# Spreading projections, experts' outputs and combining over the row maxima's units, in a TensorE queue written out by hand

## The reference

```python
slots = einsum('bsd,bset->betd', xn, softmax(logits, axis=1))
processed = gelu(slots @ w1) @ w2
out = einsum('bnd,bsn->bsd', processed, softmax(logits.reshape(b, s, e*t)))
```

## Time and profile before

| | |
|---|---|
| median of 3 runs | 1322.0 us (1321.63 to 1325.11) |
| profiled execution's own time | 1320.49 us |
| its span, first to last instruction | 1318.7 us |
| mean granted TensorE clock | 0.938 of full |
| busy: TensorE, VectorE, ACT, GpSimd | 1137.4, 908.6, 641.3, 480.9 us |
| window 388.1 to 473.4 (slot 4) | TensorE busy 79.14 us, clock 1.00 |
| window 301.6 to 388.1 (slot 3) | TensorE busy 80.55 us, clock 0.98 |

### The profile page before, as it was taken

How to read it: one execution, slowest core, us unless ns; L and a number is a source line. 1 busy time by engine, 2 the same in 40 slices (tenths; PEclk the granted TensorE clock), 3 DMA queues, 4 the chain that set the end, 5 groups by cost and what they waited for, 6 DMA issues and landing times.

```text
span 1318.7 us, 19164 instructions
## 1 busy us (share of the span) xinstructions
PE 1137.4 (86%) x6056; PEld 603.7 (46%) x6056; DVE 908.6 (69%) x2097; ACT 641.3 (49%) x1258; POOL 480.9 (36%) x602
## 2 busy tenths in 40 slices
PE   5979889999898998989996851177999999999997
PEld 3434454553554544635444430133455555455453
DVE  3627537456588687786875577998799898898131
ACT  2161734726637457385373410333465556645642
POOL 3040311312334144252333243354537546556310
PEclk8989999899999999999899885588999999999999
DMA  4220110221322314124113058221020220200000
GB/s 116 71 90 32 49 64 10 74 73 35 113 67 69 111 33 146 42 49 134 47 37 73 20 143 204 69 51 37 22 67 17 51 67 8 58 24 8 25 9 8
DMA packets 86004, 79.84 MB, mean 61 GB/s; under 512 B 43056, under 2 KB 63664, under 8 KB 83888
## 3 DMA queue, kind: packets, MB, share of 16 engines
q1 hardware_dynamic: 85936, 79.01, 22.2%
HBM read 43.17 MB, written 35.00 MB: 59 GB/s over the span
## 4 chain that ended last, share of the span: by engine, by line
PE 60%; DVE 16%; issue 9%; ACT 8%; POOL 4%; DMA 2%; SPq 1%; ACTq 0%; DVEq 0%; POOLq 0%
PE ps L1348 15%; PE ps L1329 8%; PE ps L992 5%; PE ps L957 4%; PE ps L1031 4%; ACT arena L1482 3%; PE ps L995 3%; PE ps L1339 3%; PE ps L1002 3%; PE ps L1018 3%; ACT arena L1443 2%; DVE arena L1881 2%; PE ps L1060 2%; PE ps L1098 2%; PE ps L1080 2%
## 5 line engine op out<-in xcount | busy, mean ns | idle before, releaser
L1881 DVE TENSOR_REDUCE arena<-ps 128x4 f32<-128x512 f32 (+2 forms) x192 | 197.7, 1043 | 64.0 <-PE ps L995 60.9
L1348 PE MATMUL ps<-arena,late 128*128 128x512 f32 x512 | 227.1, 596 | 0.3 <-ACT arena L1631 0.3
L1443 ACT ACTIVATE arena<-ps 128x512 f32<-128x512 f32 (+2 forms) x200 | 110.4, 569 | 210.6 <-PE ps L957 99.0
L776 POOL TENSOR_SCALAR_AFFINE_SELECT arena<-arena 128x512 f32<-128x512 f32 x128 | 90.5, 710 | 265.9 <-ACT arena L1482 265.4
L1482 ACT ACTIVATE arena<-ps 128x1024 f32<-128x1024 f32 (+3 forms) x256 | 169.3, 713 | 31.0 <-PE ps L1018 29.7
L1348 PEld LDWEIGHTS ps<-arena,late 128*128 128x128 f32 x512 | 96.3, 192 | 114.4 <-issue 112.1
L1631 ACT ACTIVATE arena<-ps,f_s 128x512 f32<-128x512 f32 x128 | 83.3, 688 | 109.3 <-PE ps L1348 98.6
L1002 PE MATMUL ps<-mask_qk,ident_b 128*128 128x512 bf16 x388 | 103.9, 388 | 25.8 <-DVE arena L2165 25.8
L1443 ACT ACTIVATE arena<-ps,arena 128x128 f32<-128x128 f32 (+1 forms) x128 | 62.3, 528 | 120.6 <-DVE arena L1908 47.2
L957 PE MATMUL ps<-ident,arena 128*128 128x128 f32 (+1 forms) x624 | 102.2, 298 | 21.6 <-ACT arena L1443 12.6
L874 POOL TENSOR_TENSOR arena<-arena 128x256 f32<-128x256 f32 x128 | 93.5, 730 | 66.0 <-ACT e_w L1690 43.3
(11 more groups left out here) (187 smaller groups left out, 1941.7 us busy)
## 6 DMA issues: line engine op xcount, KB each, us to landing
qr<-q_rep SPq DMA_DIRECT2D x16, 512.0 KB, 5.0
kr<-k_rep SPq DMA_DIRECT2D x16, 512.0 KB, 5.9
scan_d<-late SPq DMA_DIRECT2D x56, 138.0 KB, 3.0
arena<-scan_d SPq DMA_DIRECT2D x12, 552.0 KB, 7.3
q_rep<-hilo SPq DMA_DIRECT2D x24, 256.0 KB, 3.2
k_rep<-hilo SPq DMA_DIRECT2D x24, 256.0 KB, 3.5
proj_d<-arena SPq DMA_DIRECT2D x8, 768.0 KB, 5.1
late<-proj_d SPq DMA_DIRECT2D x8, 768.0 KB, 4.4
```

Source lines behind the costliest of these rows:

```text
L776: g.affine_select(out=block, in_=block, compare_op=ALU.is_ge, fill=0.0, base=0, pattern=[[0, 4], [1, P]], channel_multiplier=-1).then_inc( ...
L1348: last = pe.matmul(ps[:, ring2.bank(f"{n}{c}"), :], w[:, k, c * P:(c + 1) * P], src[:, k, :], start=(k == 0), stop=(k == HC - 1))
L1443: return act.activation(dst, src(ps[:, bank, :]), func, **kw)
L1881: v.tensor_reduce(heads[:, 2 * pr:2 * pr + 2, gs[0]:gs[-1] + 1], ps[:, at:at + 2, 0:len(gs) * w].rearrange("p q (n w) -> p q n w", w=w), X ...
```

## The change

TensorE's end of a slot is driven by a table. `UNITS_TO` says how many units are issued ahead of each of twelve pieces: c0 behind x1, c1 behind x2, c2 behind x4, c3 behind x5, the four experts' outputs (now one block each) behind x7, x8, x10 and x11, the four blocks of combining behind x12, x13, x15 and x17. The transposes of the maxima stand behind x13 as before, those of x1 behind x15 (X_AT = 16), now with combining blocks 0 and 1 ahead of them and 2 and 3 behind. Unread matmuls are issued in this stretch only in a slot without a mixture. Banks 4 and 5 change places for part of the shared uses, and xT moves from 4 to 7. ACT issues the one-element exponential and `take_x1` ahead of `take_combined`.

```diff
--- before.py
+++ after.py
@@ -40,6 +40,8 @@
 QUARTER = NC // 4
 X_LATE = 19
 NM_AT, XR_AT = 13, 14
+X_AT = 16
+UNITS_TO = [2, 3, 5, 6, 8, 9, 11, 12, 13, 14, 16, 18]
 SCW = TS * 2 * HD + 2 * HD * TS + NC * 10
 PAIRS = [(r, r * (r + 1) // 2) for r in range(CH)]
 LN_EPS = 1e-5
@@ -471,10 +473,10 @@
         assert len(turns) % 2 == 0
 
 
-        shared = [(F, "xT", 4), (T, "L0", 5), (T, "L1", 7), (T, "L2", 4), (F, "qkv0", 5), (XE, beside[0], 7), (F, "qkv1", 4),
+        shared = [(F, "xT", 7), (T, "L0", 5), (T, "L1", 7), (T, "L2", 4), (F, "qkv0", 5), (XE, beside[0], 7), (F, "qkv1", 4),
                   (F, "qkv2", 5), (XE, beside[1], 7), (F, "qkv3", 4), (T, "L3", 5), (XE, beside[2], 7), (T, "M0", 4),
                   (T, "M1", 5), (XE, beside[3], 7), (T, "M2", 4), (T, "M3", 5)]
-        shared += [(hand, use, (7, 4, 5)[k % 3]) for k, (hand, use) in enumerate([
+        shared += [(hand, use, (7, 5, 4)[k % 3]) for k, (hand, use) in enumerate([
             (K, "nm1"), (T, "cT0"), (T, "cT1"), (F, "qT"), (F, "kT"), (T, "cT2"), (T, "cT3"), (N1, "pv0"), (T, "dT0"),
             (T, "dT1"), (T, "dT2"), (T, "dT3"), (T, "sn"), (N1, "pv1"), (T, "slots"), (N1, "pv2"), (T, "h0"), (N1, "pv3"),
             (T, "h1"), (N1, "aT"), (T, "h2"), (T, "h3"), (G, "x2T"), (N1, "ao"), (G, "c0"), (G, "c1"), (G, "c2"), (G, "c3"),
@@ -1238,33 +1240,27 @@
                     nonlocal x_at
                     while x_at < end:
                         if front is not None:
-                            if x_at > NM_AT or chain_only:
+                            if chain_only:
                                 idle_matmuls(2)
                             scores_for_maxima(front, f"x{x_at}", turn)
                         x_at += 1
 
-                maxima_to(2)
-                for j in range(4):
-                    if tail is not None:
-                        project(tail, turn, j)
-                    maxima_to(3 + j)
-                for half in range(2):
-                    if moe is not None:
-                        expert_out(moe, turn, (2 * half, 2 * half + 1))
-                    maxima_to(8 + 2 * half)
-                for t in range(NT):
-                    if moe is not None:
-                        combine(moe, turn, (t,))
-                    maxima_to(11 + t)
-                if front is not None:
-                    transpose_maxima(front, turn, 0)
-                maxima_to(X_LATE - 3)
-                if b is not None:
-                    if front is not None:
-                        idle_matmuls(2)
-                    transpose_x1(b, turn)
+                pieces = [lambda j=j: project(tail, turn, j) for j in range(4)] if tail is not None else [None] * 4
+                pieces += [lambda n=n: expert_out(moe, turn, (n,)) for n in range(4)] if moe is not None else [None] * 4
+                pieces += [lambda t=t: combine(moe, turn, (t,)) for t in range(NT)] if moe is not None else [None] * 4
+                filled = moe is not None
+                for end, piece in zip(UNITS_TO, pieces):
+                    maxima_to(end)
+                    if end == NM_AT + 1 and front is not None:
+                        transpose_maxima(front, turn, 0)
+                    if end == X_AT and b is not None:
+                        if front is not None and not filled:
+                            idle_matmuls(2)
+                        transpose_x1(b, turn)
+                    if piece is not None:
+                        piece()
                 maxima_to(X_LATE)
-                if front is not None:
+                if front is not None and not filled:
                     idle_matmuls(4)
                 return now
 
@@ -1605,10 +1601,11 @@
                     take_projections(tail)
                 if moe is not None:
                     take_expert_out(moe)
+                if b is not None:
+                    act.activation(warm[:, :], ident[:, 0:1], ACT.Exp)
+                    take_x1(b)
+                if moe is not None:
                     take_combined(moe)
-                if b is not None:
-                    take_x1(b)
-                    act.activation(warm[:, :], ident[:, 0:1], ACT.Exp)
 
             take_xT(0)
             for t in range(NT):
```

## The result

The changed kernel took 1330.68 us (median of 11 runs, 1324.53 to 1342.58); the kernel before took 1324.02 us in the runs beside it (11 runs, 1321.63 to 1332.95). The ratio is 1.0061, with a 95% interval of 1.0033 to 1.0090, so the change makes the kernel slower, by 4 to 12 us on 1324. The forecast was 5.0 us; the medians differ by 6.7 us. The changed kernel's median lies 3.7 us over the predicted 1327.0. The profiled execution spans 1328.9 us, 10.2 more than the one before.

A forecast was written before the change was run, and what follows sets the result against it. TensorE was taken to bound the slot's end, busy without a break. Terms -20.4 + 18.8 + 6.6 gave +5.0 us, 1327.0 on the median of 1322.0; own range 1323.5 to 1330, over all cases 1314 to 1333.

The forecast's parts named there:

- Unread matmuls removed and pieces respread: Ends of slots 1 to 6: 16 unread matmuls fewer on TensorE's chain, 3.4 us gained a slot, -20.4 us in all.
- nothing is lost by their absence as cover of the clock: End of slot 4: the clock stays up without the unread matmuls, because real matmuls fill the stretch; no cost.
- What becomes late: Start of slots 4 to 7: the fold waits for scale_heads behind GpSimd's add; 4.0 us in slots 4 to 6; sum +18.8.
- Products longer by 1.03 us: Fold's three VectorE products, slots 4 to 6: 2.72 us beside GpSimd's score_products instead of 1.69; TensorE's new wait 4.6 us.
- e21: TensorE's unit behind the fold, ahead of projections and scores: forecast to wait 4.6 us in slots 4 to 6, 5.0 in slot 7.
- The clock, 2.2 us a slot: Slots 4 to 6, behind TensorE's stop at e21: the clock falls to 0.50, 2.2 us each, +6.6 us.
- a rival with 0.11: Clock falls again in mid-slot in slots 4 to 6, or VectorE bounds the respread units: +10 to +12 us, chance 0.11.
- Slot 7 pays it already: Slot 7: its clock already falls before the change, so no clock cost added; its forecast loss is 5.0 us.
- Slots 1 to 3: These slots have no fold waiting and keep the whole gain of 3.4 us each.
- The prediction's 3.7 us: Fold's three products by the skill's whole-instruction exclusion: 3.7 us, sum 4 us worse; the prediction went by 2.72 instead.

## Why the prediction was right, and where its sizes were off

The direction and the mechanism held: the fold waits behind the add, TensorE waits behind the fold, the clock falls behind that, and it comes to more than the removal gains. The size came out near (5.0 us forecast, 4 to 12 measured), though 1330.68 lies just over the forecast's own range of 1323.5 to 1330, and in part it came out by luck: some terms were too large, others too small.

- *Unread matmuls removed and pieces respread, -3.4 us a slot.* From x0 to L0 the timelines give 28.18 and 24.84 us in slot 4: 3.34. But "nothing is lost by their absence as cover of the clock" holds only with the respreading; alone the removal loses the clock (1335.57 us). I had asked whether VectorE keeps up in the new order, not what the old order would do without them. The lighter L1816 was right: 1.1 us in slots where GpSimd's add no longer lies beside it.
- *What becomes late, 4.0 us at the fold.* Measured 3.70 (VectorE reached the fold 0.2 us later behind L0 than before, by small waits at the tops), and 4.26 in slot 7 (4.4 worked out). Taking the wait away turned the loss into a gain: shown.
- *Products longer by 1.03 us.* Mis-sized: 1.88 us in slots 4 to 6, only 0.19 more. In slot 7 they took 2.71, as the row of slot 7's end said. The two steps behind them (0.90 and 0.74 us instead of 0.41 and 0.42) lie beside two instructions of GpSimd's L778 here, and TensorE doesn't wait for them. By the timelines e21 starts 12.29 us behind L0 in slot 4 instead of 8.38, a delay of 3.91 us, not 4.6; in slot 7 13.61 instead of 8.64, 4.97 us, as forecast.
- *The clock, 2.2 us a slot.* By the profiles the fall behind the stop costs 2.4 us a slot (the kernel with 16 matmuls). But I had put the second fall, 17 us later, into a rival with 0.11, and it came in all three slots. Its price is about 1 us a slot, as an estimate: the slots lost 11.8 us, and 3 × (3.91 + 2.4 - 3.34) = 8.9 of it are the terms above. "Slot 7 pays it already" was wrong too: its clock was low 20.5 us instead of 6.8, and the slot lost 7.1 us, not 5.0, although TensorE's delay there was as forecast.
- *Slots 1 to 3* gained 9.4 of 10.2 us, but not by 3.4 each: slot 1 gained nothing, its clock was low for 20.4 us instead of 6.8, and slot 2 gained 6.8, as its clock didn't fall any more, after 13.6 us low. That the three add up to the forecast is luck.

Why the fold's products took 1.88 us and not 2.72 shows when VectorE's and GpSimd's are taken one by one. In slot 4 of the changed kernel:

```profile
387.22 0.29 DVE L1989 TENSOR_TENSOR late<-late 128x128 f32<-128x128 f32 x1 [3.70 <-POOL late L804]
387.26 0.56 POOL L815 TENSOR_TENSOR late<-late 128x128 f32<-128x128 f32 x1
387.43 0.68 DVE L1989 TENSOR_TENSOR late<-late 128x256 f32<-128x256 f32 x1
387.79 0.91 POOL L815 TENSOR_TENSOR late<-late 128x256 f32<-128x256 f32 x1
388.03 1.08 DVE L1989 TENSOR_TENSOR late<-late 128x384 f32<-128x384 f32 x1
388.65 1.30 POOL L815 TENSOR_TENSOR late<-late 128x384 f32<-128x384 f32 x1
```

They end in turn (387.51, 387.82, 388.11, 388.70, 389.11, 389.95), each stretched by the one before it on the other engine. VectorE starts first here, by 0.04 us, and its first product is free (0.29 us); in slot 7 GpSimd starts first, by 0.03 us (655.03 against 655.06), VectorE's first product takes 0.58 us, and the three wait for three of GpSimd's instead of two. This agrees with the Trainium skill's exclusion for a whole instruction (SBUF — State Buffer, Who interferes with whom). The prediction's 3.7 us worked out from it, an estimate, was too high all the same. GpSimd's four products grow from 128 to 512 elements a partition; their mean, 0.83 us, was taken for the three shortest, which took 0.45, 0.73 and 0.99 us in the kernel before, and in slots 4 to 6 only two of them stand in VectorE's way.

The sum by slots: -9.4 (1 to 3; -10.2 forecast), +11.8 (4 to 6; +10.2 forecast), +7.1 (7; +5.0 forecast), so +9.4 between the L0 of slot 1 and of slot 8, in one profile of each kernel. Why the clock falls in some slots and holds in others with the same pauses I can't say from these runs; single profiles differ by several us in slots 0 and 1 for this alone.

## What to carry to other kernels

When work is moved later on one engine to balance it, follow its result through every queue behind it: here an add that had been harmless in GpSimd's queue carried an unrelated stage's five products with it, and reordering that queue turned a loss of 0.6% into a gain of 0.5%. Before unread matmuls are taken out, ask what TensorE will do in their place: if it waits, they may hold the clock, and the best kernel here took them out where real work fills the gap and put five in where nothing does.

## What the runs showed of the hardware

- In the kernel with the removal alone the granted clock fell from 1.00 to 0.50 at the ends of slots 1 to 6 with no stop of TensorE longer than 1.20 us in those ends (at the end of slot 4 its pauses were 1.11, 0.47, 0.47 and 0.21 us). The prediction's clock term counted only the fall behind a stop of several us.
- VectorE's and GpSimd's products, two operands in SBUF each, took turns instruction by instruction. The same three VectorE instructions took 1.1 to 1.2 us with none of GpSimd's beside them (the removal alone), 1.69 where they met only the end of GpSimd's last, 1.88 where VectorE started 0.04 us first, 2.71 where GpSimd started 0.03 us first, and 2.93 where they met the two longest of GpSimd's; GpSimd's four took 3.32 alone, but for that end, and 3.9 beside VectorE.
